# Output, fc2 and down products with row tiles as the stationary operand, sums kept by rows on top of x

## What is computed

```
a = layernorm(x)
q = a @ Wq                      (32 heads of 128)
k, v = [context; a] @ Wk, Wv    (4 key/value heads, 8 query heads each)
x = x + (softmax(q k^T / sqrt(128)) v) @ Wo
h = layernorm(x)
shared = relu(h @ up)^2 @ down                       (1024 -> 2048 -> 1024)
w = sum of the 2 largest of h @ gate                 (8 logits a row)
routed = ((h @ fc1) @ expert * w) @ fc2              (1024 -> 512 -> 512 -> 1024)
x = x + layernorm(shared + routed) * gamma + beta
```

## Time and profile before

| | us |
|---|---|
| three runs, median | 1827.82 |
| lowest to highest | 1826.76 to 1828.19 |
| the profiled execution, its own time | 1825.77 |
| its span, first to last instruction | 1824.0 |
| mean granted TensorE clock | 0.994 of full speed |
| PE busy | 1788.4 (98%) |
| DVE, ACT, POOL busy | 737.5, 647.7, 746.6 |

### The profile page before, as it was taken

The page is one execution under the profiler, slowest core; times in us unless marked ns, Lnnn a source line. Parts: engine busy times, 40 slices in busy tenths (PEclk is TensorE's granted clock), DMA queues, the critical chain, the costliest instruction groups (busy, mean ns, idle before and its releaser), DMA issues.

```text
span 1824.0 us, 27488 instructions
## 1 busy us (share of the span) xinstructions
PE 1788.4 (98%) x9254; PEld 1611.7 (88%) x9254; DVE 737.5 (40%) x1239; ACT 647.7 (36%) x1256; POOL 746.6 (41%) x539
## 2 busy tenths in 40 slices
PE   8999989999999999999999999999999999999996
PEld 7988978789999989989989999899888989889886
DVE  3611112633343367416741673177254422212226
ACT  4221212233343367415741673167322213212311
POOL 2455342245555455523542354244465322222242
PEclk9999999999999999999999999999999999999998
DMA  9878876256677554413432253233344121111134
GB/s 293 256 270 268 265 244 222 81 184 227 209 241 239 182 191 155 131 59 114 138 119 85 88 166 102 77 99 124 113 165 150 58 104 57 56 48 58 54 99 170
DMA packets 127409, 271.95 MB, mean 149 GB/s; under 512 B 17024, under 2 KB 75392, under 8 KB 124416
## 3 DMA queue, kind: packets, MB, share of 16 engines
q1 hardware_dynamic: 127360, 271.29, 45.4%
HBM read 185.57 MB, written 85.69 MB: 149 GB/s over the span
## 4 chain that ended last, share of the span: by engine, by line
PE 55%; issue 26%; POOL 14%; DMA 2%; DVE 1%; ACT 1%; POOLq 1%; SPq 0%; ACTq 0%; DVEq 0%
PE bank L1369 18%; PE bank L1371 17%; PE bank L1370 17%; POOL tile_region L713 7%; POOL slab_raw L679 3%; POOL act_region L668 2%; POOL slab_split L654 2%; PE bank L1562 1%; DMA slab_raw<-in_slabs 1%; DMA weight_sums_scratch<-slab_raw 1%; PE bank L1399 1%; DMA k_ctx_scratch<-small_region 1%; ACT slab_split L755 0%; PE bank L1428 0%; DVE small L1031 0%
## 5 line engine op out<-in xcount | busy, mean ns | idle before, releaser
L654 POOL TENSOR_TENSOR slab_split<-slab_raw,slab_split 128x1024 fp32r<-128x1024 f32 x94 | 225.2, 2395 | 463.7 <-ACT slab_split L755 463.7
L1369 PE MATMUL bank<-act_region,slab_split 128*128 128x512 f32 (+2 forms) x992 | 360.7, 364 | 1.6 <-DVE mid_region L1024 1.2
L1371 PE MATMUL bank<-act_region,slab_split 128*128 128x512 f32 (+2 forms) x992 | 360.7, 364 | 0.0
L1370 PE MATMUL bank<-act_region,slab_split 128*128 128x512 f32 (+2 forms) x992 | 360.3, 363 | 0.0
L713 POOL TENSOR_TENSOR tile_region<-tile_region,small 128x487 f32<-128x487 f32 x224 | 216.3, 1002 | 206.2 <-DVE small L1139 206.2
L755 ACT ACTIVATE slab_split<-slab_raw 128x1024 fp32r<-128x1024 f32 x94 | 99.4, 1058 | 378.6 <-PE bank L1371 378.5
L1176 DVE TENSOR_TENSOR y_region<-y_region,bank 128x512 f32 (+2 forms) x96 | 59.6, 621 | 365.5 <-PE bank L1371 365.5
L1369 PEld LDWEIGHTS bank<-act_region,slab_split 128*128 128x128 f32 x992 | 186.3, 188 | 22.8 <-issue 2.3
L1370 PEld LDWEIGHTS bank<-act_region,slab_split 128*128 128x128 f32 x992 | 186.2, 188 | 19.7
L1371 PEld LDWEIGHTS bank<-act_region,slab_split 128*128 128x128 f32 x992 | 186.2, 188 | 18.9
L1369 PE MATMUL bank<-mid_region 128*128 128x488 f32 (+2 forms) x480 | 198.6, 414 | 0.5 <-DVE mid_region L1163 0.5
(11 more groups left out here) (147 smaller groups left out, 3021.5 us busy)
## 6 DMA issues: line engine op xcount, KB each, us to landing
slab_raw<-in_slabs SPq DMA_DIRECT2D x126, 512.0 KB, 3.6
q_scratch<-y_region SPq DMA_DIRECT2D x16, 1792.0 KB, 8.1
mid_region<-q_scratch SPq DMA_DIRECT2D x32, 896.0 KB, 5.6
weight_sums_scratch<-slab_raw SPq DMA_DIRECT2D x16, 1024.0 KB, 3.9
v_scratch<-slab_split SPq DMA_DIRECT2D x8, 1536.0 KB, 9.2
slab_raw<-weight_sums_scratch SPq DMA_DIRECT2D x48, 256.0 KB, 4.6
mid_region<-v_scratch SPq DMA_DIRECT2D x32, 384.0 KB, 3.2
k_ctx_scratch<-small_region SPq DMA_DIRECT2D x32, 375.0 KB, 7.9
```

The lines of the kernel that those rows point to most:

```text
L654: pool.tensor_tensor(WS[s][1], RAWS[s], f32(WS[s][0]), ALU.subtract).then_inc(s_wlo, 1)
L1369: pe.matmul(out_ap, w[0], a[0], start=first, stop=False)
L1370: pe.matmul(out_ap, w[0], a[1], start=False, stop=False)
L1371: return pe.matmul(out_ap, w[1], a[0], start=False, stop=last)
```

## The change

The output, fc2 and down products hold a 128 x 128 tile of the activations (one row tile, one 128-deep step) as the stationary operand and move weights, 512 output columns wide, past it (`row_product`). Results come with rows on partitions. `Y` now lies by rows and starts as x, which SP loads during the first head group's attention (`load_y`) in place of POOL's zeroing. So the groups "y" and "z" are gone, and with them the second pass over slabs: `SEG2` and what follows take 50 slabs (positions 24 to 73).

A slab of these products is now two 128-deep steps by 512 columns, gathered by one DMA from four pieces of 256 columns (1 KB each) in every partition (`row_slab`, `fc2_slab`); the moving operand of a matmul is four pieces of 128 columns, 256 apart. For every slab there are 7 groups of 6 matmuls, one for each row tile, and 7 adds of 128 x 512 on DVE. The last four slabs of the last Wo and of the last down products are taken in pairs, row tile by row tile (`wo_last`, `down_last`: 12 matmuls a group, two groups a row tile), as are fc2's four, so that each row tile ends early. Statistics are taken from `Y` by halves as these groups end.

There are four slab slots from position 24 on (`slot_of`): two old ones, the region of the k buffers, and the tail of the attention's region. A slab takes its slot when the slab four before it is done with; ACT's split of it stands in its list where that slab ends (`done_with`).

In the logits the gate's high and low parts lie side by side in one stationary tile: two matmuls a step. w is applied to rows where DVE takes fc2 out of the bank. At the end POOL applies gamma and adds x2 + beta (`x_beta_scratch`) for row tiles 0 to 5, and DVE does it for row tile 6 by halves, each stored when it is done. The core of the diff:

```diff
-P_FC1 = P_SEG2 + 2 * NK
-P_EXP = P_FC1 + 2 * (LAT // P)
+P_FC1 = P_SEG2 + NK
+P_EXP = P_FC1 + LAT // P
 P_FC2 = P_EXP + LAT // P // 2
-P_FFN = P_FC2 + HID // P // 2
+P_FFN = P_FC2 + 4
 P_SEG3 = P_FFN + 3 * NK
-N_POS = P_SEG3 + 2 * NK
-assert N_POS == len(SLAB_AT)
+N_POS = P_SEG3 + NK
...
+ROW_SLABS = ((0, 0), (0, 1), (1, 0), (1, 1), (2, 0), (3, 0), (2, 1), (3, 1))
+FC2_SLABS = ((0, 0), (1, 0), (0, 1), (1, 1))
...
+def slot_of(p):
+    return p % 2 if p < P_SEG2 else (p - P_SEG2) % 4
+
+
+def row_products(what, p0):
+
+
+    single = [(what, r, ROW_SLABS[a][1], (p0 + a,)) for a in range(4) for r in range(RT)]
+    paired = [[(what + "_last", r, eh, (p0 + 4 + 2 * eh, p0 + 5 + 2 * eh)) for eh in range(2)] for r in range(RT)]
+    return single, paired
...
+WO_SINGLE, WO_PAIRED = row_products("wo", P_SEG2)
+SEG2 = WO_SINGLE + WO_PAIRED[0] + [g for r in range(1, RT) for g in WO_PAIRED[r] + both("n", r - 1)] + weave(
+    [("fc1", m, 0, (P_FC1 + m,)) for m in range(4)], {0: both("n", RT - 1)}) + [
+    ("fc1", m, 1, (P_FC1 + m,)) for m in range(4)] + [("logit", 0), ("logit", 1)] + weave(
+    [("exp", m, h, (P_EXP + m // 2,)) for m in range(4) for h in range(2)], {0: [("logitT", 0)]}) + [
+    ("fc2", r, eh, (P_FC2 + 2 * eh, P_FC2 + 2 * eh + 1)) for eh in range(2) for r in range(RT)]
+DOWN1 = [("down", r, eh, (P_FFN + NK + a,)) for a, (kp, eh) in enumerate(ROW_SLABS) for r in range(RT)]
+DOWN_SINGLE, DOWN_PAIRED = row_products("down", P_SEG3)
+SEG3 = DOWN_SINGLE + [g for r in range(RT) for g in DOWN_PAIRED[r]]
...
+        WS += [[part(RD, l * SLAB, SLAB) for l in range(2)], [part(RB, 2 * NK * ROWS + l * SLAB, SLAB) for l in range(2)]]
...
+            def row_slab(first, a):
+
+                kp, eh = ROW_SLABS[a]
+                return slabs[first + 4 * eh:first + 4 * eh + 4, :, 2 * P * kp:2 * P * (kp + 1)].rearrange("m p c -> p m c")
...
+            ended = done_with(SEG2)
             for j, g in enumerate(SEG2):
-                if j in turns:
-                    next_slab(turns[j])
+                for p in ended.get(j, []):
+                    next_slab(p + 6)
...
+                for p in ended.get(j, []):
+                    next_lo(p + 4)
+                if g[0] == "wo_last" and g[2] == 1:
                     r = g[1]
                     pool.wait_ge(s_xn, B + r + 1)
-                    pool.tensor_tensor(XIN[r % 2], XIN[r % 2], BETA, ALU.add).then_inc(s_x2b, 1)
-            slabs_lo(P_FFN + 1, N_POS - P_FFN - 2)
-            slab_lo(N_POS - 1, 1)
+                    pool.tensor_tensor(Y[:, r, :], Y[:, r, :], BETA, ALU.add).then_inc(s_x2b, 1)
...
+            pool.wait_ge(s_gamma, 16)
+            for r in range(RT - 1):
+                pool.wait_ge(s_xn, B + RT + r + 1)
+                pool.tensor_tensor(Y[:, r, :], Y[:, r, :], GAMMA, ALU.mult).then_inc(s_gm, 1)
+                pool.wait_ge(s_gm, r + 1)
+                pool.wait_ge(s_xin[r % 3], 16 * (r // 3 + 1))
+                pool.tensor_tensor(Y[:, r, :], Y[:, r, :], XB[r % 3], ALU.add).then_inc(s_o, 1)
...
+                for p in ended.get(j, []):
+                    next_hi(p + 4, c + 1)
...
-            def add_to_y(c, c_static, m, h):
+            def add_to_y(c, c_static, r, eh):
                 dve.wait_ge(s_mm, c + 1)
-                cols = slice(*PARTS[h])
-                dve.tensor_tensor(Y[:, m, cols], Y[:, m, cols], gb(c_static)[:, 0:PARTS[h][1] - PARTS[h][0]],
-                                  ALU.add).then_inc(s_ev, 1)
-
-            def y_slabs(c0, c_static):
-                with dve.Fori(0, NK // 2) as i:
-                    for s in range(2):
-                        for h in range(2):
-                            add_to_y(c0 + 4 * i + 2 * s + h, c_static + 2 * s + h, 2 * i + s, h)
+                dve.tensor_tensor(Y[:, r, cols_of(eh)], Y[:, r, cols_of(eh)], gb(c_static)[:, :], ALU.add).then_inc(s_ev, 1)
...
+            def half_stats(c, r, eh):
+
+                dve.wait_ge(s_ev, c + 1)
+                return dve.bn_stats(stats[:, 6 * eh:6 * eh + 6], Y[:, r, cols_of(eh)])
...
+            for j, g in enumerate(SEG3):
+                c, r, eh = C_SEG3 + j, g[1], g[2]
+                add_to_y(c, c, r, eh)
+                if g[0] == "down_last":
+                    n = B + RT + r
+                    rows_mean_var(c, r, eh, n)
+                    if eh == 1 and r < RT - 1:
+                        normalise(r, n, Y[:, r, :], Y[:, r, :])
...
+            for eh in range(2):
+                half = Y[:, r, cols_of(eh)]
+                link(dve.scalar_tensor_tensor(out=half, in0=half, scalar=mv[:, r, 0:1], in1=GAMMA[:, cols_of(eh)],
+                                              op0=ALU.subtract, op1=ALU.mult))
+                dve.scalar_tensor_tensor(out=half, in0=half, scalar=rs[:, r:r + 1], in1=XB[r % 3][:, cols_of(eh)],
+                                         op0=ALU.mult, op1=ALU.add).then_inc(s_oh, 1)
...
+            def row_product(c, c_static, slabs_of, acts, r):
+
+                bank_free(c)
+                last_k = len(slabs_of) - 1
+                for a, (w, k0) in enumerate(slabs_of):
+                    for k in range(2):
+                        last = three(gb(c_static)[:, :], [acts(l, k0 + k, r) for l in range(2)],
+                                     [w[l].rearrange("p (m k c) -> p m k c", m=4, k=2)[:, :, k, :] for l in range(2)], a == k == 0, a == last_k and k == 1)
+                last.then_inc(s_mm, 1)
...
+                for j, (kp, eh) in enumerate(ROW_SLABS):
+                    pe.wait_ge(s_wlo, P_WO + kv * NK + j + 1)
+                    for r in range(RT):
+                        if j == 0:
+                            attention_rows(kv, r)
+                        row_product(C_WO + kv * N_ROWS + RT * j + r, C_WO + RT * j + r, [(WS[j % 2], 2 * kp)],
+                                    rows_of_attention, r)
```

542 lines of the change are left out of this document (234 added, 308 removed).

## The result

The changed kernel took 1795.55 us in the median of four runs (1794.98 to 1797.2), the kernel before beside it 1828.01 (1826.76 to 1829.62): ratio 0.9823, 95% interval 0.9806 to 0.984. Forecast were 1798.4 us in a range of 1791 to 1809, and faster with 0.91. The profiled execution took 1795.56, its span 1793.6 against 1824.0, so 30.4 us went; the prediction's sum had 29.4. The median came out 2.85 us lower than forecast: 1.0 of it is this difference in the sum, and nearly all the rest is that the profiled execution stood at its kernel's median here, where the one before had stood 2.05 under it.

The account below looks back on a forecast made before the run. PE, busy for 98% of the span, was taken to set the time. Terms of -1.8, -14.0, -0.6 and -13.0 summed to -29.4 us, giving a span of 1794.6 and a median of 1798.4 us, range 1791 to 1809.

Parts of the forecast that it names:

- step 2: From the last output products to the first up slab: 190.6 us against 204.7, new waits included, -14.0 us.
- step 4: Last down layer and tail: products 76.7, a wait of 1.05 and a tail of 8.4, 86.2 against 99.15, -13.0 us.
- step 1: Turned products, three head groups in the loop: 42 wide matmuls a slab, 76.7 us for 77.3 each, -1.8 us.
- step 3: The three layers up, down, up: only down changes, 76.7 us for 77.3, -0.6 us.
- costly groups: Rival: every matmul group costs 0.04 us beyond its matmuls, 9.7 us more, 1808 us; chance 0.10.
- pair wait: Last slabs in pairs: PE waits 1.05 us for slab 7's split, covered by only one group of 12 matmuls.
- first fc1 wait: Start of fc1: PE waits 1.15 us for slab 0's split, which stands behind POOL's adding of beta for row tile 5.
- the second: Behind fc1's first group: PE waits 2.75 us for row tile 5's transposes, as ACT stands at slab 2's load.
- E: The end of the last matmul, from which the tail was counted: E + 8.2 us, tail 8.4 with POOL's wait.
- Moving operand in pieces: Rival: each break in the turned products' moving operand costs 13 ns, 85 us in all, 1884 us; chance 0.07.
- Slow slab loads: Rival: slab loads in 1 KB pieces hold PE up, which needs four times the 3.6 us load; chance 0.03.
- DVE and POOL taking turns: Rival: DVE's scaling always follows POOL's two steps; tail grows 1 to 2 us, fc1's start as much, 1801; chance 0.06.

Follow-up runs that it names:

- a0: The changed kernel itself, run again unaltered as the mark for the other runs; 1790.07 us, ratio 0.9827 to the kernel before.
- e2: Changed kernel with the first two row tiles' pair groups crossed, so two groups cover each split; 1794.73 us, ratio 0.9842 to the kernel before.
- e5: As e1, with POOL's addition of beta for row tile 5 also behind its splits of fc1's slabs; 1788.43 us, ratio 0.9819 to the kernel before.
- e1: Changed kernel with ACT's splits of fc1's slabs 2 and 3 put behind row tile 5's high parts; 1784.62 us, ratio 0.9792 to the kernel before.
- e3: Changed kernel with the turned products' moving operand as one run of 512 columns, computing another product; 1791.55 us, ratio 0.9837 to the kernel before.
- e7: e5 plus e2's pair order, row tile 0's transposes one group later, gamma moved from POOL to DVE, deviation's reciprocal to ACT; 1781.82 us, ratio 0.9789 to the kernel before.
- best version: The kernel of e7, run again beside the changed kernel in the same rounds: 1782.15 us against 1787.59, ratio 0.9774 to the kernel before.

## Why the prediction was right

The mechanisms were those forecast, but for the clock in step 2 and for POOL's lag in step 4, and the sum, 29.4 for 30.4, owes part of its closeness to errors that cancel: steps 1, 3 and 4 gained 1.6, 0.6 and 0.3 us more than forecast, and step 2 gained 1.6 less. No run takes the 14 us of step 2 apart into the "y" and routing transposes, the logits' third matmul and PE's old waits; that these are gone is read from the trace.

**Prices and groups.** 42 matmuls were forecast at 0.228, and took 0.2267: 9.52 us a slab, in groups of 6. The 0.01 us a group that was put into the price does not exist, nor does the 0.04 of the rival "costly groups"; the half-size groups of the earlier trace rows had paid for the change of width between them. That is the whole miss of step 1, -3.4 for -1.8, and of step 3, -1.2 for -0.6.

**Step 2.** a0 without the clock's fall gives 190.62 for 190.6, but two small errors cancel in it. The products were 0.3 us dearer than counted: every group right behind transposes takes about 0.1 us longer (in the first trace from 1335.76 to 1338.58, 2.82 for 2.72), which outweighed the cheaper matmul. The waits were cheaper by as much: 1.11, 1.13 and 2.45 for 1.05, 1.15 and 2.75. Their causes are shown one by one: the pair wait is the split's 3.8 us over one group's cover (e2 gives two groups and it is gone), the first fc1 wait is POOL's beta (e5), the second is ACT standing at a load (e1). What failed in the first profile is a term that the sum lacked: 1.6 to 1.7 us of half clock behind the longest wait.

**Step 4.** 85.81 for 86.2. Behind E the output steps took 3.43 (0.75 each, and 0.45 of waiting for POOL) where 2.85 had been put, and the last store landed 2.44 after the last step where 3.07 had been taken from the earlier trace rows; these cancel as well. DVE's scaling grew from 0.94 to 1.21 over five row tiles, so POOL's lag does add up, by about 0.07 us a row tile, which the text had denied. It is harmless with the pair wait in place, and costs 1.9 us without it (e2).

**The rivals.** Costly groups: refuted by 0.2267. Moving operand in pieces: refuted by e3. Slow slab loads: refuted by 3.4 us. DVE and POOL taking turns: true as a mechanism and small here. The Trainium skill ("SBUF - State Buffer", section "SBUF: two separate sides") has a DVE instruction with two SBUF inputs take the lock too, against a GpSimd instruction that reads SBUF. This case's traces agree: the step at 1787.73 took 1.20 beside POOL and 0.75 in e7, where POOL's last step was over, while the adds, with one input in a bank, took 0.69 beside POOL.

**The margin.** The best version lay 5.4 us further down. It is made of the waits that the prediction had priced one by one (1.05 twice, 1.15 and 2.75), but for 0.37 us of the third, which the best version still has, and of the clock's fall behind the last of them.

## What to carry to other kernels

When a product is turned so that its results come out by rows, price the matmuls by columns and look for the gain in what it removes behind them; then see that the last slabs end row tile by row tile, or the tail takes it back (20.6 us of 30.4 here). A wait's bracket names the last engine of a chain: ask what the engine before it stood at in its own list, since a slab split that waits for a load blocks the small step behind it (2.5 us, and the clock besides). Before a short wait is removed, look whether it feeds a queue that runs at nearly PE's pace: here 1.3 us gained on PE came back as 1.9 in the tail until POOL had half its work taken away.

## What the runs showed of the hardware

- At one place TensorE's granted clock stood at half (1.2 GHz) for 3 to 4 us behind an idle stretch of 2.05 to 3.67 us in six traces, and held at 2.4 GHz behind 1.90 and 1.96. At another it fell behind 1.89 to 1.91 us in six traces and held behind 1.89 or 1.90 in eight, and at a third it held behind 2.36. The fall cost 1.6 to 1.7 us in the first place.
- A moving operand in four pieces of 128 columns, 256 apart, runs at the same 0.2267 us as one run of 512.
- Groups of 6 matmuls cost nothing beyond their matmuls (0.2267 us each, as in groups of 24); a group right behind transposes costs about 0.1 us.
- DVE blocked by POOL ends 0.55 us after POOL's instruction, whatever its own length was to be, both with one SBUF input (3.00 for 0.81 in e2) and with two (1.20 for 0.75).
- In one trace (e2) the stretch from 400 to 600 us, at a granted clock of 1.00, held 970 matmul records where all others hold 988 or 989: 2% slower with nothing in the profile to name it. It lies before all that the change touches, and was left open.
